# First FFN matmul of a dense top-2 MoE block: weights loaded one chunk at a time, and the two token halves of a chunk interleaved

## The chip, the cores and the metric

One Trainium2 chip, 8 cores. Each core runs the same program on its own batch element (x has the shape 8 x 2048 x 1024); the cores share nothing but read the same weights. The metric is the device time of the slowest core, in microseconds (us). TensorE is PE in the rows, VectorE DVE, ScalarE ACT, GpSimd POOL and SyncE SP.

## The reference

Each token is normalised, goes through an attention block whose softmax weights the token's own value (so it is a value projection and an output projection), and through a mixture of 8 experts with top-2 routing. Every expert is computed for every token; the routing weights pick two of them afterwards.

```python
def _L0_ffn_ref(hidden_states, router_w, w1, b1, w2, b2):
    router_logits = jnp.einsum('bth,eh->bte', x, router_w)
    topk_values, topk_indices = jax.lax.top_k(router_logits, TOP_K)
    topk_weights = jax.nn.softmax(topk_values.astype(jnp.float32), axis=-1).astype(x.dtype)
    h1 = jnp.einsum('bth,efh->btef', x, w1) + b1
    h1 = jax.nn.gelu(h1, approximate=False)
    expert_outputs = jnp.einsum('btef,ehf->bteh', h1, w2) + b2
    ...
xn = _layernorm(x, axis=-1)
x = x + _L0_attn_ref(xn, ...) + _L0_ffn_ref(xn, ...)
```

Per core: 2048 tokens, width 1024, 8 experts, inner width 4096.

## The kernel before

The program is written as five streams of instructions, one for each engine, with semaphores between them that the code sets by hand (class Plan, lines 26 to 65). The order on each engine is the order in which the code emits. All matmuls are bf16 into fp32 PSUM; the weights lie in memory as fp32 and are cast to bf16 by the DMAs that POOL issues.

**Stages.** emit_A (line 210) normalises 128 tokens, transposes them into xnF and computes the routing weights; it runs 16 times. emit_vproj (line 169) is the value projection, once for four tiles of tokens. The FFN goes over two halves of 1024 tokens, and in each half over the 8 experts e. For one half and one expert, emit_h1 (line 355) computes h1 in 16 groups g of two chunks f1c (32 chunks of 128 inner columns), and emit_w2 (line 386) then takes those chunks through w2 in two sweeps hh of 512 output columns each. In the first half, expert 0's 16 groups of h1 are mixed between the calls of emit_A for the tiles 8 to 15 (lines 475 to 479). emit_outproj (line 359) stands before w2 of expert 0 in each half. emit_final (line 447) adds x and the result and stores it; its loads and stores are issued by SP.

**One group of h1, emit_h1_group, line 316.** One DMA on POOL's queue (line 321) loads both chunks of the group: 128 partitions x 2 chunks x 1024 values, 512 KB as they arrive in bf16, into one of two slots of w1sl (slot g % 2, 2048 columns each). Before it, POOL waits until the last matmul that read this slot is done (line 319). Each chunk then has 16 matmuls (line 338): 8 slices fc of the width 1024, for each of two halves j of the 1024 tokens, 512 tokens each. The stationary operand is the 128x128 block fc of the chunk's weights, the moving one 512 tokens of xnF, and j names the PSUM bank of the chunk's pair of banks (SP[f1c % 2], P01 or P23). j is the outer loop and fc the inner one, so the 8 blocks are gone through once for j = 0 and once more for j = 1. Before the first matmul of a chunk, PE waits for the DMA (line 328), for ACT to have read the pair two chunks earlier (wait_pair, line 329), and where needed for the readers of vg (line 333). Behind the last matmul ACT takes Gelu over both banks into vg (line 350).

**One group of w2, line 389.** One 256 KB DMA (line 396) into one of four slots, then 2 chunks x 8 token tiles = 16 matmuls (line 419), each into one of the eight PSUM banks, with another stationary block for every matmul.

**emit_outproj** (line 369) has fc outer and j inner: the same stationary block of optF stands in two matmuls one after the other, which write the two banks of a pair.

POOL's queue holds, in this order, the w1 DMAs of an expert, the w2 DMAs of both sweeps, the w1 DMAs of the next expert, and so on; a DMA that waits holds up all behind it.

Of the kernel before, what the change touches and what calls it, by code (L numbers as in the profile page):

```python
# [17 lines left out]
NFC = 8  # L18
# [49 lines left out]
def build_nc(phases="ABC", dbg=False):  # L68
# [8 lines left out]
    d_w1 = nc.dram_tensor("w1r", [E, NF1C, 128, NFC, 128], F32, kind="ExternalInput").ap()  # L77
# [14 lines left out]
    w1sl = wvw[:, 0:4096]  # L92
# [15 lines left out]
    if dbg:  # L108
# [12 lines left out]

    p = Plan(nc)
    p.mksem("pe", "act", "dve", "dx0", "dx1", "dq0", "dq1", "dw1a", "dw1b",
            "dw2a", "dw2b", "dw2c", "dw2d", "dcst", "dwv", "dwo", "do0", "do1",
            "ddbg")
    DX = ("dx0", "dx1")
    DQ = ("dq0", "dq1")
    DW1 = ("dw1a", "dw1b")
    DW2 = ("dw2a", "dw2b", "dw2c", "dw2d")
    DO = ("do0", "do1")  # L130

# [10 lines left out]
    for fc in range(NFC):  # L142
        p.do("gpsimd", lambda g, fc=fc: g.dma_start(
            wo_sb[:, fc * 1024:(fc + 1) * 1024], d_wo[fc * 128:(fc + 1) * 128, :]),
            inc="dwo", inc_by=16)
# [12 lines left out]
    def wait_pair(pidx):  # L158
        if pair_last[pidx] is not None:
            sem, tok = pair_last[pidx]  # L160
            p.wait("tensor", sem, tok)

    def set_pair(pidx, sem, tok):
        pair_last[pidx] = (sem, tok)
# [136 lines left out]
            emit_vproj(tt // 4)  # L301


    nw1 = {0: 0, 1: 0}
    nw2 = {0: 0, 1: 0, 2: 0, 3: 0}
    tok_w1use = {}
    tok_w2use = {}
# [6 lines left out]
    tok_w2_reader = {}  # L314

    def emit_h1_group(half, e, g):
        sl = g % 2
        if tok_w1use.get(sl) is not None:
            p.wait("gpsimd", "pe", tok_w1use[sl])
        nw1[sl] += 1  # L320
        p.do("gpsimd", lambda gg, e=e, g=g, sl=sl: gg.dma_start(  # L321
            w1sl[:, sl * 2048:(sl + 1) * 2048].rearrange(
                "p (c m) -> p c m", c=2),
            d_w1[e, 2 * g:2 * g + 2].rearrange("c p f n -> p c (f n)")),
            inc=DW1[sl], inc_by=16)
        for f1c in (2 * g, 2 * g + 1):
            pair = SP[f1c % 2]
            p.wait("tensor", DW1[sl], 16 * nw1[sl])
            wait_pair(f1c % 2)
            if e == 0 and half == 0:  # L330
                p.wait("tensor", "dve", tok_xnFev[7])
            if tok_w2_reader.get(f1c) is not None:
                p.wait("tensor", "pe", tok_w2_reader[f1c])
            for j in range(2):
                for fc in range(NFC):
                    tok = p.do("tensor",
                               lambda t, fc=fc, f1c=f1c, j=j, sl=sl, half=half,
                               pair=pair: t.matmul(  # L338
                                   pair[:, j * 512:(j + 1) * 512],
                                   w1sl[:, sl * 2048 + (f1c % 2) * 1024 +  # L340
                                        fc * 128: sl * 2048 + (f1c % 2) * 1024 +
                                        fc * 128 + 128],
                                   xnF[:, fc * T + half * 1024 + j * 512:
                                       fc * T + half * 1024 + (j + 1) * 512],
                                   start=(fc == 0), stop=(fc == NFC - 1)),
                               inc=("pe" if (j == 1 and fc == NFC - 1) else None))
            tok_w1use[sl] = tok
            p.wait("scalar", "pe", tok)
            tok_gelu[(half, e, f1c)] = p.do(
                "scalar", lambda s, f1c=f1c, e=e, pair=pair: s.activation(  # L350
                    vg[:, f1c * 1024:(f1c + 1) * 1024], pair, AF.Gelu,
                    bias=b1c_sb[:, f1c * E + e: f1c * E + e + 1]), inc="act")
            set_pair(f1c % 2, "act", tok_gelu[(half, e, f1c)])

    def emit_h1(half, e):
        for g in range(NF1C // 2):
            emit_h1_group(half, e, g)
# [117 lines left out]
    for tt in range(8, NTT):  # L475
        if DO_C:
            emit_h1_group(0, 0, 2 * (tt - 8))
            emit_h1_group(0, 0, 2 * (tt - 8) + 1)
        emit_A(tt)
# [14 lines left out]
    if dbg:  # L494
# [6 lines left out]
        for dst, s_ in dumps:  # L501
            p.do("gpsimd", lambda g, dst=dst, s_=s_: g.dma_start(dst, s_),
                 inc="ddbg", inc_by=16)
# [75 lines left out]
```

How the kernel before makes its waits and increments, by code:

```python
    def wait(self, eng, name, val=None):  # L40
        v = self.cnt[name] if val is None else val
        if v <= 0 or self.waited[eng].get(name, -1) >= v:
            return
        self.waited[eng][name] = v
        s = self.sem[name]
        self.streams[eng].append(lambda En, s=s, v=v: En.wait_ge(s, v))
# [3 lines left out]
    def do(self, eng, fn, inc=None, inc_by=1):  # L50
        own = self.SELF_SEM.get(eng)
        if own is not None:
            self.wait(eng, own)
            if inc is None:
                inc, inc_by = own, 1
        if inc is None:
            self.streams[eng].append(fn)
            return None
        self.cnt[inc] += inc_by
        tok = self.cnt[inc]
        s = self.sem[inc]
        self.streams[eng].append(
            lambda En, fn=fn, s=s, n=inc_by: fn(En).then_inc(s, n)
        )
        return tok
```

## Time and profile before

| what | value |
|---|---|
| runs shown | 4741.36 and 4861.77 us, median 4801.57 us |
| the profiled execution | 4190.35 us, of which its span (first to last instruction of the slowest core, core 5) is 4188.8 us |
| spans of the 8 cores | 4149.0 to 4188.8 us |
| mean granted TensorE clock | 0.957 on core 5, 0.957 to 0.966 over the cores |
| PE busy | 3809.2 us, 91% of the span |
| POOL busy | 575.3 us, 14% |
| DMA | 307.02 MB moved, 73 GB/s on the mean |

The profile is of one execution, on the slowest of its cores. Matmuls are pipelined, and the end of each is modelled: one takes 379 ns in the records, but the next starts 216 ns after it. Idle time counts only where the engine with the work waits; for this kernel that is PE.

### The profile page before, as it was taken

What the parts mean: (1) busy time and instruction counts of PE and PEld (TensorE: products, weight loads), DVE (VectorE), ACT (ScalarE), POOL (GpSimd) and SP (SyncE); (2) the same over time, 40 slices, a digit from 0 to 9 for tenths busy, and PEclk for the clock granted to TensorE, in tenths of its full rate; (3) what the DMA queues carried; (4) which work ended last, traced back from release to release, by engine and by line L of the source; (5) the groups of instructions that cost most, each with busy time, mean ns of one, the idle gap of its engine ahead of it and who ended that gap; (6) DMA issues with size and microseconds to landing.
All of it is one profiled execution on the core that took longest, in us unless ns stands there. A gap on an engine that the chain in (4) does not pass through costs nothing.

```text
span 4188.8 us, 41300 instructions; the slowest of 8 cores (4149.0 to 4188.8 us)
## 1 busy us (share of the span) xinstructions
PE 3809.2 (91%) x17200; PEld 1692.3 (40%) x17200; DVE 372.6 (9%) x626; ACT 626.8 (15%) x610; POOL 575.3 (14%) x817
## 2 busy tenths in 40 slices
PE   3456799999999999999999999999999999999994
PEld 1222344444444444444444444444444444444442
DVE  3331100000001010000001000000000010100001
ACT  0122103021111202030201103020111202030200
POOL 1001010111111111111111011111111111111110
PEclk9677899999999999999999999999999999999986
DMA  4334254544454544544456354445454444454443
GB/s 75 53 54 73 29 78 66 73 74 73 74 78 71 76 70 76 78 71 71 76 73 138 62 75 75 69 73 74 74 77 72 77 69 76 72 81 67 75 67 99
DMA packets 251605, 307.02 MB, mean 73 GB/s; under 512 B 47591, under 2 KB 178663, under 8 KB 251424
## 3 DMA queue, kind: packets, MB, share of 16 engines
q0 software_dynamic: 244512, 279.21, 45.2%
q1 hardware_dynamic: 6912, 25.17, 1.8%
q8 instruction: 141, 2.31, 0.2%
q14 instruction: 40, 0.33, 0.0%
HBM read 574.89 MB, written 8.39 MB: 139 GB/s over the span
## 4 chain that ended last, share of the span: by engine, by line
PE 84%; DMA 6%; DVE 6%; issue 2%; ACT 1%; DVEq 0%; POOL 0%; SPq 0%; ACTq 0%; POOLq 0%
PE P L419 41%; PE P L338 39%; DMA wvw<-w1r 4%; DVE scr L433 3%; PE P L369 1%; PE P L188 1%; DMA wvw<-wvf 1%; PE P L247 1%; DMA x_rot<-x 1%; ACT vg L350 1%; DVE xnF L253 0%; DMA b1c_sb<-b1c 0%; DVE scr L239 0%; DVEq L46 0%; ACT L232 0%
## 5 line engine op out<-in xcount | busy, mean ns | idle before, releaser
L419 PE MATMUL P<-wvw,vg 128*128 128x512 bf16 x8192 | 1833.1, 385 | 65.0 <-DVE scr L433 49.2
L338 PE MATMUL P<-xnF,wvw 128*128 128x512 bf16 x8192 | 1787.6, 381 | 29.4 <-DMA wvw<-w1r 22.5
L419 PEld LDWEIGHTS P<-wvw,vg 128*128 128x128 bf16 x8192 | 806.7, 99 | 1088.8 <-issue 201.2
L338 PEld LDWEIGHTS P<-xnF,wvw 128*128 128x128 bf16 x8192 | 800.4, 98 | 1014.9 <-issue 66.4
L350 ACT ACTIVATE vg<-P,b1c_sb 128x1024 bf16<-128x1024 f32 x512 | 570.5, 1114 | 2876.1 <-PE P L338 2876.0
L396 POOL DMA_DIRECT2D wvw<-w2r x512 | 359.8, 705 | 1600.8 <-PE P L419 1535.0
L433 DVE SCALAR_TENSOR_TENSOR scr<-P,wmap_sb,scr 128x512 f32<-128x512 f32 x256 | 192.1, 750 | 3284.6 <-PE P L419 3260.5
L321 POOL DMA_DIRECT2D wvw<-w1r x256 | 180.0, 704 | 1664.1 <-PE P L338 1664.1
L188 PE MATMUL P<-xnF,wvw 128*128 128x512 bf16 x256 | 85.1, 501 | 40.6 <-DMA wvw<-wvf 40.6
L247 PE MATMUL P<-scr 128*128 128x128 f32 x128 | 30.0, 413 | 98.2 <-DVE scr L239 80.9
L188 PEld LDWEIGHTS P<-xnF,wvw 128*128 128x128 bf16 x256 | 29.4, 120 | 94.6 <-issue 83.0
L294 PE MATMUL P<-scr,wmap_sb 128*8 128x128 f32 x16 | 5.9, 372 | 66.6 <-DVE wmap_sb L290 66.6
L178 POOL DMA_DIRECT2D wvw<-wvf x32 | 28.2, 885 | 278.3 <-PE P L188 278.3
L247 PEld LDWEIGHTS P<-scr 128*128 128x128 f32 x128 | 24.1, 216 | 104.5 <-issue 104.5
L369 PE MATMUL P<-wo_sb,optF 128*128 128x512 bf16 x256 | 58.0, 380 | 1.0 <-ACT optF L197 1.0
L350 ACT ACT_TABLE_LOAD x9 | 11.5, 1283 | 207.1 <-PE P L338 207.1
L197 ACT ACTIVATE optF<-P,bvc_sb 128x512 bf16<-128x512 f32 x32 | 22.0, 687 | 114.6 <-PE P L188 114.6
L369 PEld LDWEIGHTS P<-wo_sb,optF 128*128 128x128 bf16 x256 | 23.8, 98 | 34.1 <-issue 7.4
L382 DVE COPY scr<-P 128x1024 f32<-128x1024 f32 x16 | 19.6, 1225 | 140.9 <-PE P L375 140.9
L239 DVE TENSOR_SCALAR scr<-x_rot,scr 128x1024 f32<-128x1024 f32 x16 | 13.0, 812 | 206.0 <-ACT scr L234 206.0
L262 PE MATMUL P<-rout_sb,xnF 128*128 128x8 bf16 x128 | 5.7, 168 | 25.4 <-DVE xnF L253 25.4
L294 PEld LDWEIGHTS P<-scr,wmap_sb 128*8 128x8 f32 x16 | 1.3, 83 | 67.5 <-issue 67.5
(40 smaller groups left out, 194.7 us busy)
## 6 DMA issues: line engine op xcount, KB each, us to landing
wvw<-w1r POOLq DMA_DIRECT2D x256, 512.0 KB, 5.2
wvw<-w2r POOLq DMA_DIRECT2D x512, 256.0 KB, 4.2
x_rot<-x SPq DMA_DIRECT2D x32, 512.0 KB, 4.3
wvw<-wvf POOLq DMA_DIRECT2D x32, 256.0 KB, 4.8
out<-x_rot SPq DMA_DIRECT2D x16, 512.0 KB, 3.6
wo_sb<-wo POOLq DMA_DIRECT2D x8, 256.0 KB, 11.0
b1c_sb<-b1c POOLq DMA_DIRECT2D x1, 128.0 KB, 12.8
scr<-iden POOLq DMA_DIRECT2D x1, 64.0 KB, 6.1
```

Of the source, the lines that this page charges most:

```text
L178: p.do("gpsimd", lambda g, vc=vc, sl=sl: g.dma_start(wvf_sl[:, sl * 1024:(sl + 1) * 1024].rearrange("p (c n) -> p c n", c=NFC), d_wvf[vc]. ...
L188: t.matmul(vps, wvf_sl[:, sl * 1024 + fc * 128: sl * 1024 + (fc + 1) * 128], xnF[:, fc * T + ts * 512: fc * T + (ts + 1) * 512], start=(fc ...
L197: s.activation(optF[:, vc * T + ts * 512: vc * T + (ts + 1) * 512], vps, AF.Identity, bias=bvc_sb[:, vc:vc + 1]), inc="act")
L247: tok = p.do("tensor", lambda t, fc=fc, xnt_t=xnt_t: t.transpose(P67[:, fc * 128:(fc + 1) * 128], xnt_t[:, fc * 128:(fc + 1) * 128], iden_ ...
L321: p.do("gpsimd", lambda gg, e=e, g=g, sl=sl: gg.dma_start(w1sl[:, sl * 2048:(sl + 1) * 2048].rearrange("p (c m) -> p c m", c=2), d_w1[e, 2 ...
L338: pair=pair: t.matmul(pair[:, j * 512:(j + 1) * 512], w1sl[:, sl * 2048 + (f1c % 2) * 1024 + fc * 128: sl * 2048 + (f1c % 2) * 1024 + fc * ...
L350: "scalar", lambda s, f1c=f1c, e=e, pair=pair: s.activation(vg[:, f1c * 1024:(f1c + 1) * 1024], pair, AF.Gelu, bias=b1c_sb[:, f1c * E + e: ...
L369: p.do("tensor", lambda t, fc=fc, tt=tt, j=j, pair=pair: t.matmul(pair[:, j * 512:(j + 1) * 512], optF[:, fc * T + tt * 128: fc * T + (tt ...
L382: v.tensor_copy(mixed[:, tl * 1024:(tl + 1) * 1024], pair), inc="dve")
L396: p.do("gpsimd", lambda gg, e=e, g=g, hh=hh, sl=sl: gg.dma_start(w2sl[:, sl * 1024:(sl + 1) * 1024].rearrange("p (c n) -> p c n", c=2), d_ ...
L419: t.matmul(W2B[tl], vg[:, f1c * 1024 + tl * 128: f1c * 1024 + (tl + 1) * 128], w2sl[:, sl * 1024 + (f1c % 2) * 512: sl * 1024 + (f1c % 2) ...
L433: v.scalar_tensor_tensor(mixed[:, tl * 1024 + hh * 512: tl * 1024 + hh * 512 + 512], W2B[tl], wmap_sb[:, tt * E + e: tt * E + e + 1], mixe ...
```

## The change

The change does three things, all in emit_h1_group.

- The DMA of a group is cut into two, one for each chunk, 256 KB each, and w1sl into four slots of 1024 columns (slot f1c % 4) with a semaphore each (dw1a to dw1d). The bytes in SBUF are as before. Each DMA waits for the last reader of its own slot, four chunks earlier; both DMAs of a group are issued ahead of the group's matmuls in the code.
- PE waits for each chunk's own DMA.
- The loops over fc and j change places: fc is outer, j inner, so that one stationary block stands in two matmuls one after the other.

```diff
+    DW1 = ("dw1a", "dw1b", "dw1c", "dw1d")
     def emit_h1_group(half, e, g):
-        sl = g % 2
-        if tok_w1use.get(sl) is not None:
-            p.wait("gpsimd", "pe", tok_w1use[sl])
-        nw1[sl] += 1
-        p.do("gpsimd", lambda gg, e=e, g=g, sl=sl: gg.dma_start(
-            w1sl[:, sl * 2048:(sl + 1) * 2048].rearrange(
-                "p (c m) -> p c m", c=2),
-            d_w1[e, 2 * g:2 * g + 2].rearrange("c p f n -> p c (f n)")),
-            inc=DW1[sl], inc_by=16)
         for f1c in (2 * g, 2 * g + 1):
+            sl = f1c % 4
+            if tok_w1use.get(sl) is not None:
+                p.wait("gpsimd", "pe", tok_w1use[sl])
+            nw1[sl] += 1
+            p.do("gpsimd", lambda gg, e=e, f1c=f1c, sl=sl: gg.dma_start(
+                w1sl[:, sl * 1024:(sl + 1) * 1024],
+                d_w1[e, f1c].rearrange("p f n -> p (f n)")),
+                inc=DW1[sl], inc_by=16)
+        for f1c in (2 * g, 2 * g + 1):
+            sl = f1c % 4
             pair = SP[f1c % 2]
             p.wait("tensor", DW1[sl], 16 * nw1[sl])
...
-            for j in range(2):
-                for fc in range(NFC):
+            for fc in range(NFC):
+                for j in range(2):
                     tok = p.do("tensor",
...
-                                   w1sl[:, sl * 2048 + (f1c % 2) * 1024 +
-                                        fc * 128: sl * 2048 + (f1c % 2) * 1024 +
-                                        fc * 128 + 128],
+                                   w1sl[:, sl * 1024 + fc * 128:
+                                        sl * 1024 + fc * 128 + 128],
```

On PE this is the beginning of h1 of expert 1 in the first half, right behind the w2 sweeps of expert 0. dw1a to dw1d are the semaphores of the w1 DMAs, dve those of the last sweep's sums, act the Gelus, pe the readers of vg. Before:

```order
L338 MATMUL P<-xnF,wvw 128x512 [waits dw1a,dve]
L338 MATMUL P<-xnF,wvw 128x512 x15
L338 MATMUL P<-xnF,wvw 128x512 [waits dve,pe]
L338 MATMUL P<-xnF,wvw 128x512 x15
L338 MATMUL P<-xnF,wvw 128x512 [waits dw1b,act]
L338 MATMUL P<-xnF,wvw 128x512 x15
L338 MATMUL P<-xnF,wvw 128x512 [waits act,pe]
L338 MATMUL P<-xnF,wvw 128x512 x15
```

The same place in the changed kernel, where the matmul's line is 339:

```order
L339 MATMUL P<-xnF,wvw 128x512 [waits dw1a,dve]
L339 MATMUL P<-xnF,wvw 128x512 x15
L339 MATMUL P<-xnF,wvw 128x512 [waits dw1b,dve,pe]
L339 MATMUL P<-xnF,wvw 128x512 x15
L339 MATMUL P<-xnF,wvw 128x512 [waits dw1c,act]
L339 MATMUL P<-xnF,wvw 128x512 x15
L339 MATMUL P<-xnF,wvw 128x512 [waits dw1d,act,pe]
L339 MATMUL P<-xnF,wvw 128x512 x15
```

Every chunk of 16 matmuls, and not every second, now waits for a DMA; the number of matmuls and their shapes stay.

On POOL this is the end of a w2 sweep pair, the w1 DMAs of the next expert, and the beginning of its w2. Before:

```order
L396 DMA wvw<-w2r 128x2x512
L396 DMA wvw<-w2r 128x2x512 [waits pe] x28
L321 DMA wvw<-w1r 128x2x1024 x2
L321 DMA wvw<-w1r 128x2x1024 [waits pe] x14
L396 DMA wvw<-w2r 128x2x512 x4
L396 DMA wvw<-w2r 128x2x512 [waits pe] x28
```

And in the changed kernel, where the DMA's line is 322:

```order
L396 DMA wvw<-w2r 128x2x512
L396 DMA wvw<-w2r 128x2x512 [waits pe] x28
L322 DMA wvw<-w1r 128x1024 x4
L322 DMA wvw<-w1r 128x1024 [waits pe] x28
L396 DMA wvw<-w2r 128x2x512 x4
L396 DMA wvw<-w2r 128x2x512 [waits pe] x28
```

The 16 w1 DMAs of an expert become 32 of half the size; 4 in place of 2 are issued without a wait, and they hold the same four chunks. What stands before and behind them keeps its place.

## Rows read from the trace of the kernel before

**Rows 1.** The page: span, and busy time (share, count) of each engine.

```profile
span 4188.8 us, 41300 instructions; the slowest of 8 cores (4149.0 to 4188.8 us)
PE 3809.2 (91%) x17200; PEld 1692.3 (40%) x17200; DVE 372.6 (9%) x626; ACT 626.8 (15%) x610; POOL 575.3 (14%) x817
```

**Rows 2.** The page: groups; count | busy us, mean ns | idle before, releaser.

```profile
L419 PE MATMUL P<-wvw,vg 128*128 128x512 bf16 x8192 | 1833.1, 385 | 65.0 <-DVE scr L433 49.2
L338 PE MATMUL P<-xnF,wvw 128*128 128x512 bf16 x8192 | 1787.6, 381 | 29.4 <-DMA wvw<-w1r 22.5
...
L338 PEld LDWEIGHTS P<-xnF,wvw 128*128 128x128 bf16 x8192 | 800.4, 98 | 1014.9 <-issue 66.4
...
L321 POOL DMA_DIRECT2D wvw<-w1r x256 | 180.0, 704 | 1664.1 <-PE P L338 1664.1
...
L369 PE MATMUL P<-wo_sb,optF 128*128 128x512 bf16 x256 | 58.0, 380 | 1.0 <-ACT optF L197 1.0
...
L369 PEld LDWEIGHTS P<-wo_sb,optF 128*128 128x128 bf16 x256 | 23.8, 98 | 34.1 <-issue 7.4
```

**Rows 3.** The waits of core 5: who <- for whom: us, times, longest.

```profile
PE P L419 <- DVE scr L433: 49.2, 95, 1.1
...
PE P L338 <- DMA wvw<-w1r: 22.5, 26, 2.6
```

**Rows 4.** The waits of core 1, whose span is 4149.0 us.

```profile
PE P L338 <- DMA wvw<-w1r: 9.4, 13, 1.7
```

**Rows 5.** Timeline, 632 to 662 us: h1 of expert 1; idle before in brackets.

```profile
632.01 13.97 PE L338 MATMUL P<-xnF,wvw 128*128 128x512 bf16 x64 [0.77 <-DVE scr L433]
...
639.63 0.70 POOL L321 DMA_DIRECT2D wvw<-w1r  x1 [19.53 <-PE P L338]
...
646.28 14.09 PE L338 MATMUL P<-xnF,wvw 128*128 128x512 bf16 x64 [0.30 <-DMA wvw<-w1r]
646.53 0.71 POOL L321 DMA_DIRECT2D wvw<-w1r  x1 [6.20 <-PE P L338]
```

**Rows 6.** Timeline, 478 to 500 us: PE in emit_outproj.

```profile
479.87 3.61 PE L369 MATMUL P<-wo_sb,optF 128*128 128x512 bf16 x16 [0.98 <-ACT optF L197]
```

**Rows 7.** The w1 DMAs by their line: who waited, and issue to landing.

```profile
L321 POOL DMA_DIRECT2D wvw<-w1r x256: 696/707/737, 188.4 to 3987.5; - x128
...
  PE P L338: 22.5, 26
...
DMA to landing us min/median/max: 5.0/5.2/9.3
```

**Rows 8.** The w2 DMAs the same way; nothing stands under "who waited".

```profile
L396 POOL DMA_DIRECT2D wvw<-w2r x512: 696/707/745, 472.0 to 4119.1; - x171
...
who waited for it (us, times):
busy tenths in 40 slices 0000010101010010101010010101010010101010
DMA to landing us min/median/max: 3.9/4.2/8.9
```

**Rows 9.** Timeline, 2228 to 2345 us: h1 at the start of the second half.

```profile
2280.75 0.70 POOL L321 DMA_DIRECT2D wvw<-w1r  x1 [8.23 <-PE P L338]
...
2287.65 0.71 POOL L321 DMA_DIRECT2D wvw<-w1r  x1 [6.21 <-PE P L338]
2289.65 0.61 PEld L338 LDWEIGHTS P<-xnF,wvw 128*128 128x128 bf16 x4 [3.04 <-issue]
2289.68 15.66 PE L338 MATMUL P<-xnF,wvw 128*128 128x512 bf16 x64 [2.57 <-DMA wvw<-w1r]
```

**Rows 10.** Windows of core 5, PE alone: busy (count), granted clock, DMA share, GB/s.

```profile
868.00:954.00 86.00, 86.00 (x400) 1.00 0.47 74
4075.00:4130.00 55.00, 55.00 (x212) 0.81 0.40 57
2281.00:2289.00 8.00, 6.10 (x29) 1.00 0.82 192
2290.00:2293.00 3.00, 3.00 (x9) 0.52 0.89 160
```

**Rows 11.** The chain that ended last, in order of time: start, us, what.

```profile
3773.16 53.48 PE P L419 x247
...
4068.64 65.46 PE P L419 x244
```

More of the change, by code:

```diff
@@ L123, in build_nc @@
     p.mksem("pe", "act", "dve", "dx0", "dx1", "dq0", "dq1", "dw1a", "dw1b",
-            "dw2a", "dw2b", "dw2c", "dw2d", "dcst", "dwv", "dwo", "do0", "do1",
-            "ddbg")
+            "dw2a", "dw2b", "dw2c", "dw2d", "dw1c", "dw1d", "dcst", "dwv",
+            "dwo", "do0", "do1", "ddbg")
     DX = ("dx0", "dx1")
     DQ = ("dq0", "dq1")
-    DW1 = ("dw1a", "dw1b")
+    DW1 = ("dw1a", "dw1b", "dw1c", "dw1d")
     DW2 = ("dw2a", "dw2b", "dw2c", "dw2d")
@@ L301, in emit_A @@
             emit_vproj(tt // 4)
-    nw1 = {0: 0, 1: 0}
+    nw1 = {0: 0, 1: 0, 2: 0, 3: 0}
     nw2 = {0: 0, 1: 0, 2: 0, 3: 0}
```

## The prediction

> **What bounds the kernel now.** I read the engines' busy times first. PE is busy for 3809.2 of 4188.8 us, and no other engine reaches 16% [rows 1]. The groups then say which matmuls these are: the two FFN lines, 8192 matmuls each, hold 1833.1 and 1787.6 us [rows 2]. The change touches line 338 alone, so the question is how much slack its 1787.6 us and the idle time before it hold.
>
> A busy PE need not be at its best pace, so next comes the timeline. Where h1 runs without a stop, 64 matmuls take 13.97 us [rows 5]; the last record is some 0.38 us long [rows 2], so one starts (13.97 - 0.38) / 63 = 215.7 ns after the other. At the granted clock of 1.00, which is the level of 2.4 GHz [rows 10], 512 columns need 512 / 2.4 = 213.3 ns. The stream is within 1.2% of one column each cycle. 8192 x 215.7 ns = 1767 us, so the 1787.6 us hold about 21 us that are not pace (drains in front of waits and matmuls at the lower clock), and idle time adds 29.4 us, of which 22.5 us stand against the w1 DMA, in 26 waits [rows 2, 3]. Were all of it to go, that is 50 us or 1.2%; this is the ceiling.
>
> **The 26 waits.** A w1 DMA is issued when the slot's second chunk is done, and it is needed one group later. Two rows show it: issue at 639.63, matmuls that need it at 646.28, after 0.30 us of idle time [rows 5]. The lead is 32 x 0.2157 = 6.9 us less the tail of the last matmul. The DMA lands after 5.2 us on the median and 9.3 at worst [rows 7], so most groups are not late, and the late ones are late by little. The worst stand at the start of the second half, where SP's loads and stores of emit_final share the DMA engines: issue at 2280.75, need met at 2289.68 after 2.57 us [rows 9], at a DMA share of 0.82 against 0.47 in a quiet stretch [rows 10].
>
> **Part 1, the split DMA and four slots.** A chunk's DMA is now issued when the chunk four before it is done, and three chunks lie between: the lead is 48 x 0.2157 = 10.4 us in place of 6.9. What does a 256 KB DMA take on this queue? The w2 line answers: 512 of them with four slots, one in every 16 matmuls, landing after 4.2 us on the median and 8.9 at worst, and PE waited for none [rows 8]. That is just the scheme that w1 gets, at the same cadence of 16 x 0.2157 = 3.45 us. So I let the 26 waits go. Each had idle time, and also a pipe that ran empty: the last record before it ends 379 - 216 = 163 ns past the time at which the next would have started. So the price is 22.5 + 26 x 0.163 = 26.7 us. The longest wait, with PE idle for 2.57 us, is followed by matmuls at the lower level of 1.2 GHz (clock 0.52 over 2290 to 2293; 64 matmuls take 15.66 in place of 13.97 us) [rows 9, 10], which adds 1.7 us. I leave about 3 us standing at the start of the second half, where DMA shares of 0.82 to 0.89 say that the engines are nearly full. Gain: about 25 us. Bounds: nothing, if all waits come back, and 28 us.
>
> What is late next behind these waits? ACT's Gelu and the last sweep's sums on DVE; neither gets nearer, since each chunk still has its 16 matmuls.
>
> The Trainium skill speaks against splitting: "DMA: Bandwidth & Descriptors", section "Rules for kernel authors", wants one large transfer, because each carries a fixed cost of about 2 us. The rows agree that halving does not halve the time (5.2 to 4.2 us) [rows 7, 8]; by that rule as by the rows the fixed part lies beside matmuls, and the sum stays.
>
> **Part 2, twice the issues.** 256 more issues on POOL at 704 ns are 180 us of POOL [rows 2], which is busy for 575.3 of 4188.8 us [rows 1]; an issue every 3.45 us leaves it 2.7 us of rest. Behind a waiting w1 DMA stand the w2 DMAs of the same expert; the last w1 DMA waits for chunk 27 as before, so they start no later than by one issue. Cost on the path: nothing; were the cover gone, 180 us.
>
> **Part 3, one more DMA wait for each second chunk on PE.** It is met long before, as that for ACT is, and such waits cost nothing visible: 400 matmuls of 25 chunks fill 86.00 of 86.00 us [rows 10], 215 ns each.
>
> **Part 4, fc outside, j inside.** The order shows as many matmuls as before. Does each keep its weight load? The output projection is written in the new order already and has 256 loads for 256 matmuls [rows 2]. A load takes 98 ns beside a matmul of 216 ns and lies under it; 16 matmuls in the new order take 3.61 us, (3.61 - 0.38) / 15 = 215 ns each [rows 6], and line 419 changes bank and block with each matmul at (53.48 - 0.38) / 246 = 215.9 ns [rows 11]. So neither alternating banks nor a block that stands twice moves the pace: 0 us. Bounds: 8192 x (215.7 - 213.3) = 20 us less, if the pace fell to the column count; and 401 us more, as in the first rival.
>
> **Sum.** 4190.35 - 25 = 4165 us against the profiled execution, 0.6% less. Core 1 had only 9.4 us of these waits [rows 4], so the slower cores gain more than the faster ones; core 5 stays near the top.
>
> The runs shown have a median of 4801.57 us, 611 us above that execution, and no row shows where they spend it. One row suggests it: in the last 130 us the granted clock is 0.81 [rows 10], and there 244 matmuls take 65.46 us, 268 ns each against 216 [rows 11], that is 1.24 times as long. The excess of 551 and 671 us would be about 2300 to 2800 us of work at that pace (551 / 0.24 and 671 / 0.24): an estimate. At that pace 32 matmuls are 8.6 us, and a DMA of 5 to 7 us is not late; what the waits cost there is nearly nil. If the first 1300 to 1800 us run at full clock, the change takes out the waits of that part alone, some 9 us, and 1 or 2 us later. So I forecast 4801.57 - 11 = 4790 us.
>
> **Rivals.**
>
> *Weight loads come out from under the matmuls (slower).* Place: the second matmul of each pair, whose load finds the same block. Price: 4096 x 98 ns = 401 us, 5190 us. It decides from 2% on, 96 us, which is 12 ns for each matmul of the line. Against it stand the 16 matmuls of 3.61 us [rows 6]. The Trainium skill's "TensorE: Matmul & The Clock Gate", section "The mechanism" of its part 3, lets a load overlap only where the row groups differ; by that it would be exposed in both kernels. The trace disagrees: 98 + 216 ns would be a pace of 314. Chance 0.02.
>
> *The two small DMAs are served one after the other (slower).* Then a pair takes 2 x 4.2 = 8.4 us against 6.9 us of matmuls, 1.5 us late for each of 256 groups, 384 us: 5170 us. It decides once a chunk's DMA takes over 3.8 us of the queue for itself. Against it: w2's DMAs have the same size and cadence, and no wait [rows 8]. Chance 0.02.
>
> *The clock steps down at another time.* The step to 0.81 stood near the end of the profiled execution and would stand halfway in the runs shown. If it comes 400 us of work earlier or later, that is 96 us, and the change needs no part in it: the two runs shown differ by 120 us. Later: 4690 us or less, down to 4165 if it hardly comes; chance 0.14. Earlier: 4890 us and up to 4165 + 0.24 x 3809 = 5080; chance 0.08. The Trainium skill's "TensorE: Matmul & The Clock Gate", section "Seeing it yourself", has a peak-current limit that takes the clock to 13/16 soon after a third core of a die does dense work; by it nearly the whole run would be at 0.81, the 5080 us. The trace disagrees: clock 1.00 at 868 us with eight cores at work [rows 10].
>
> *Fewer weight loads by reuse (faster).* Were the second load of each pair gone, 4096 loads would be gone that nobody waits for: 0 us, within the forecast.
>
> **How the numbers follow.** Forecast, within 2%: 0.74, with a range of its own from 4700 to 4875. Faster by over 2%: 0.14, all of it the clock, since 50 us is the ceiling of the change itself. Slower by over 2%: 0.08 + 0.02 + 0.02 = 0.12. 2% is about what a measurement of this kernel can tell from no change; its two runs lie 2.5% apart. For 8 in 10 the range runs from 4540, half of the clock's better side, to 4890.
>
> **What would show it.** Right: PE's waits for w1 fall from 26 to 5 or fewer and below 3 us; 8192 loads remain on the h1 line and 64 matmuls still take 13.97 us; 512 w1 DMAs land after about 4.2 us; POOL's busy time rises to some 755 us; the span falls by 20 to 28 us. Wrong: a pace of h1 away from 215.7 ns at clock 1.00, DMA waits of PE at every group, or fewer loads with a shorter time.

## The result, and the profile after

The changed kernel takes 0.9932 of the time before, with a 95% interval of 0.9919 to 0.9945: faster by 0.7%, which lies within the 2% that the prediction allows its forecast. The medians are 4156.43 us (11 runs, 4150.78 to 4759.68) and 4466.99 us (10 runs, 4179.22 to 4888.12). These medians are not the comparison: in some executions of either kernel the cores of a die are granted 0.81 of TensorE's clock (the lower grant) for part of the time, and the ratio is over the executions in which that did not happen, 4150.78 to 4157.18 us against 4179.22 to 4192.62.

First the page of the changed kernel, from the profiled execution of 4150.11 us (slowest core: 7): the span, the busy times and the groups that answer to [rows 1] and [rows 2].

```profile
span 4148.6 us, 42034 instructions; the slowest of 8 cores (4134.1 to 4148.6 us)
...
PE 3790.2 (91%) x17200; PEld 1690.6 (41%) x17200; DVE 372.5 (9%) x626; ACT 626.8 (15%) x610; POOL 667.0 (16%) x1073
...
L419 PE MATMUL P<-wvw,vg 128*128 128x512 bf16 x8192 | 1818.2, 383 | 65.6 <-DVE scr L433 49.9
L339 PE MATMUL P<-xnF,wvw 128*128 128x512 bf16 x8192 | 1782.2, 381 | 6.6 <-DVE scr L433 6.6
...
L339 PEld LDWEIGHTS P<-xnF,wvw 128*128 128x128 bf16 x8192 | 802.5, 98 | 984.2 <-issue 28.3
...
L396 POOL DMA_DIRECT2D wvw<-w2r x512 | 360.1, 706 | 1586.0 <-PE P L419 1513.6
L322 POOL DMA_DIRECT2D wvw<-w1r x512 | 271.3, 533 | 1546.1 <-PE P L339 1546.1
```

The h1 line kept its 8192 matmuls and its 8192 weight loads. What went is the idle time before it: 29.4 us in [rows 2], now 6.6 us, all of it the wait for the last sweep's sums, which was there before. The wait for w1 is no longer among the releasers. The DMAs' own rows say the same (they answer to [rows 7]):

```profile
L322 POOL DMA_DIRECT2D wvw<-w1r x512: 528/528/568, 187.5 to 3963.8; - x171
...
who waited for it (us, times):
busy tenths in 40 slices 0000001010000101010100001010000001010100
DMA to landing us min/median/max: 3.9/4.2/8.5
```

They are 512 now, land after 4.2 us on the median and 8.5 at worst, and nothing stands under "who waited". On the eight cores together one wait of 0.4 us is left, on core 6; before, each core had between 9.4 and 23.6 us.

The worst place before was the start of the second half [rows 9]. The timeline of PE in the changed kernel there, 2240 to 2320 us:

```profile
2239.64 80.67 PE L339 MATMUL P<-xnF,wvw 128*128 128x512 bf16 x373
```

One unbroken row: 372 steps in 80.67 - 0.38 us, 215.8 ns each. Before, the same stretch was six pieces with five waits between them, and one piece begun at the level of 1.2 GHz.

### The profiled spans fell by more than the ratio says

The slowest core's span fell by 40.2 us (4188.8 - 4148.6); the ratio says 0.68% of 4181, which is 28 us. Core 5, the slowest before, explains the difference. Its groups in the changed kernel:

```profile
L419 PE MATMUL P<-wvw,vg 128*128 128x512 bf16 x8192 | 1815.2, 383 | 66.4 <-DVE scr L433 50.7 <-ACT vg L350 13.7 <-DVE scr L382 2.0
L339 PE MATMUL P<-xnF,wvw 128*128 128x512 bf16 x8192 | 1781.8, 380 | 6.6 <-DVE scr L433 6.6
```

On this core the h1 line gave back 1787.6 - 1781.8 = 5.8 us of busy time and 29.4 - 6.6 = 22.8 us of idle time, 28.6 us together: this is the change. It is no peculiarity of core 5: busy and idle time of the h1 line together fall from 1817.0 to 1789.4 us on the mean of the eight cores, which is 27.6 us. Line 419, which the change doesn't touch, gave another 1833.1 - 1815.2 = 17.9 us. That is the granted clock: in the kernel before, core 5 ended at 0.80, as its window from 4029 to 4135 us shows (busy, matmuls, granted clock, DMA share, GB/s). Its last h1 matmuls are over by 4001 us, so none of the 28.6 us comes from there. In the changed kernel's profile no core is below 0.91 in any 40 us from 520 to 4080 us.

```profile
4029.00:4135.00 106.00, 103.42 (x388) 0.80 0.39 54
```

### The profile page after: what moved, and what is told of

Same layout as the page of the kernel before. It is cut to its first block, busy times and chain, and to the rows that moved or that the text cites. A ratio compares the mean times of both kernels' runs of the same rounds, so it can differ in the third digit from the quotient of the medians.

```text
span 4148.6 us, 42034 instructions; the slowest of 8 cores (4134.1 to 4148.6 us)
## 1 busy us (share of the span) xinstructions
PE 3790.2 (91%) x17200; PEld 1690.6 (41%) x17200; DVE 372.5 (9%) x626; ACT 626.8 (15%) x610; POOL 667.0 (16%) x1073
## 4 chain that ended last, share of the span: by engine, by line
PE 88%; DVE 6%; DMA 2%; issue 2%; ACT 1%; DVEq 0%; POOL 0%; SPq 0%; ACTq 0%; POOLq 0%
PE P L339 43%; PE P L419 42%; DVE scr L433 3%; DMA wvw<-wvf 1%; PE P L188 1%; PE P L369 1%; DMA x_rot<-x 1%; PE P L247 1%; ACT vg L350 1%; DVE xnF L253 0%; DMA b1c_sb<-b1c 0%; DVE scr L239 0%; DVEq L46 0%; ACT L232 0%; DVE x_rot L463 0%
## 5 line engine op out<-in xcount | busy, mean ns | idle before, releaser
L322 POOL DMA_DIRECT2D wvw<-w1r x512 | 271.3, 533 | 1546.1 <-PE P L339 1546.1
L188 PE MATMUL P<-xnF,wvw 128*128 128x512 bf16 x256 | 88.5, 517 | 41.3 <-DMA wvw<-wvf 41.2
L247 PEld LDWEIGHTS P<-scr 128*128 128x128 f32 x128 | 22.5, 204 | 103.7 <-issue 103.7
```

The costliest lines, as they stand in the source:

```text
L188: t.matmul(vps, wvf_sl[:, sl * 1024 + fc * 128: sl * 1024 + (fc + 1) * 128], xnF[:, fc * T + ts * 512: fc * T + (ts + 1) * 512], start=(fc ...
L247: tok = p.do("tensor", lambda t, fc=fc, xnt_t=xnt_t: t.transpose(P67[:, fc * 128:(fc + 1) * 128], xnt_t[:, fc * 128:(fc + 1) * 128], iden_ ...
L322: p.do("gpsimd", lambda gg, e=e, f1c=f1c, sl=sl: gg.dma_start(w1sl[:, sl * 1024:(sl + 1) * 1024], d_w1[e, f1c].rearrange("p f n -> p (f n)")),
```

## The experiments

Each time is a ratio to the kernel before, run on the same chip beside it.

**The split without the changed loops.** j is outside again; the DMAs, slots and waits are the changed kernel's.

```diff
-            for fc in range(NFC):
-                for j in range(2):
+            for j in range(2):
+                for fc in range(NFC):
```

> Split DMA and four slots, with the old loop order (j outside, fc inside). If the gain is the w1 DMAs' lead (my theory): 0.993 of before, waits of PE for w1 at most 2 on core 0 to 7 and under 1 us, pace of h1 215.8 ns. If the gain comes from the same block standing in two matmuls (rival): 1.000 of before.

This run gave no ratio (its profiled execution took 4152.57 us), so the same kernel was run once more.

> The split alone (old loop order) once more with more rounds, for its ratio. If the split is the whole gain: 0.993 of before, as the changed kernel. If the loops' order has a part: nearer to 0.996.

Measured in the second: 0.9942, interval 0.9924 to 0.996, which holds the changed kernel's 0.9932; in both profiles no core has a wait for w1. The ratio alone does not separate 0.993 from 0.996. The first profile says more: busy and idle time of the h1 line together are 1790.0 us on the mean of the eight cores, where the changed kernel has 1789.4 and the kernel before 1817.0.

**The changed loops without the split.** The reverse: the kernel before with fc outside and j inside.

```diff
-            for j in range(2):
-                for fc in range(NFC):
+            for fc in range(NFC):
+                for j in range(2):
```

> Only the loops change places; one 512 KB DMA for two chunks and two slots as before. My theory: 1.000 of before within 0.002, some 13 to 28 waits for w1 and 9 to 24 us of them on a core as in the rows of before, pace 215.8 ns with 8192 loads. Rival: 0.993, and a pace below 215.8 ns.

Here, too, the first run gave no ratio, and the kernel was run once more.

> The changed loop order alone once more with more rounds. If the order is worth nothing: 1.000 of before within 0.002. If it has a part in the gain: 0.997 or less.

Measured: 1.0001, interval 0.9991 to 1.0012. The group of the h1 line in its second profile (core 3, span 4175.7 us):

```profile
L338 PE MATMUL P<-xnF,wvw 128*128 128x512 bf16 x8192 | 1785.8, 380 | 24.8 <-DMA wvw<-w1r 16.6
```

The waits for w1 are back, 16.6 us on this core and 10.0 to 17.0 us over the eight. The order of the loops is worth nothing, to within 0.1%, as its part of the sum said. In this one profile the h1 line takes 1810.6 us on the mean of the cores, 6.4 less than in the profile before, but the ratio over the timed executions shows no gain. With the split alone at the changed kernel's level, the 0.7% is the split.

**The smaller DMA, with the old lead for the first chunk.** Both DMAs of a group are held until the whole group two before it is done. The second chunk, which is needed 16 matmuls later, keeps its 10.4 us.

```diff
-            if tok_w1use.get(sl) is not None:
-                p.wait("gpsimd", "pe", tok_w1use[sl])
+            if tok_w1use.get(sl | 1) is not None:
+                p.wait("gpsimd", "pe", tok_w1use[sl | 1])
```

> The changed kernel, but both DMAs of a group are issued only when the whole group two before it is done, as the one DMA was; so the first chunk keeps the old lead of 6.9 us and the second has 10.4 us. If the lead is what counts (as the prediction put it): most of the 26 waits come back, over 12 us of them, 0.996 to 1.000 of before. If the smaller DMA with a semaphore of its own is enough (rival: 256 KB land after 4.2 us and not 5.2): under 6 us of waits, 0.993 to 0.995.

Measured: 0.995, interval 0.9932 to 0.9967. Its waits on the slowest core (7), us, times, longest, and where on the timeline they stand:

```profile
PE P L339 <- DMA wvw<-w1r: 4.3, 3, 1.9
```

```profile
2257.57 34.79 PE L339 MATMUL P<-xnF,wvw 128*128 128x512 bf16 x160 [1.74 <-DMA wvw<-w1r]
2293.03 7.07 PE L339 MATMUL P<-xnF,wvw 128*128 128x512 bf16 x32 [0.68 <-DMA wvw<-w1r]
2301.98 18.29 PE L339 MATMUL P<-xnF,wvw 128*128 128x512 bf16 x84 [1.88 <-DMA wvw<-w1r]
```

The rival is right: 0.2 to 4.3 us of waits over the cores, not over 12. With the old lead a 256 KB DMA lands after 4.8 us on the median, in time for a need 6.9 us on. It is late at the start of the second half, beside SP's loads and stores, and hardly elsewhere: of the 23 waits on the eight cores 20 stand there, and the other three, on cores 2 and 4, are 0.2 to 0.3 us long.

**The longer lead without the smaller DMA.** The kernel before with a third slot.

```diff
-    w1sl = wvw[:, 0:4096]
-    wo_sb = A("wo_sb", [128, NFC * 1024], BF16).ap()
+    w1sl = wvw[:, 0:6144]
+    wo_sb = A("wo_sb", [128, 6 * 1024], BF16).ap()
...
-        sl = g % 2
+        sl = n_group[0] % 3
+        n_group[0] += 1
```

> The kernel before with one slot more: 512 KB DMAs as before, three slots, so a lead of 32 matmuls more (13.8 us in place of 6.9). The third slot's room is taken from the output projection's weights: its last two of eight blocks are not loaded and the first two used in their place. If a longer lead alone suffices: no waits for w1 but at the start of the second half, 0.993 to 0.994 of before. If the size of the DMA is what matters (rival): waits stay near 26, 0.998 or more.

Measured: 0.994, interval 0.9919 to 0.9962. Its w1 DMAs on core 7:

```profile
L323 POOL DMA_DIRECT2D wvw<-w1r x256: 696/707/735, 188.1 to 3962.1; - x128
...
  PE P L340: 0.4, 1
...
DMA to landing us min/median/max: 5.0/6.1/14.0
```

One wait of 0.4 us; 1.5 us is the most on any core. Against the expectation none of them stands at the start of the second half: all lie before 350 us, where h1 is mixed with emit_A. The DMAs land later than before on this core (6.1 us on the median for the 5.2 of [rows 7], 14.0 at worst for 9.3); why is not shown, and it does no harm with 13.8 us to go. The ratio rests on few executions, but the h1 line itself agrees. Its busy and idle time together, in the profiled executions, on the mean of the eight cores:

| kernel | h1 line, us | waits for w1 on a core, us |
|---|---|---|
| before | 1817.0 | 9.4 to 23.6 |
| changed loops alone | 1810.6 | 10.0 to 17.0 |
| smaller DMA, old lead for the first chunk | 1792.4 | 0.2 to 4.3 |
| longer lead, 512 KB DMA | 1790.7 | 0 to 1.5 |
| split alone | 1790.0 | 0 |
| changed kernel | 1789.4 | 0 to 0.4 |

So either half of the change nearly does it alone, and the two do not add up.

**Twice as many DMAs again.** Each chunk's DMA cut in two, 128 KB each.

```diff
-            p.do("gpsimd", ...
-                w1sl[:, sl * 1024:(sl + 1) * 1024],
+            for q in range(2):
+                p.do("gpsimd", ...
+                    w1sl[:, sl * 1024 + q * 512:sl * 1024 + (q + 1) * 512],
```

> The changed kernel with each chunk's DMA cut in two once more, 128 KB each and 1024 of them in place of 512, same slots and waits. If issues and a DMA's fixed part lie beside the matmuls (my theory): 0.993 of before, no waits for w1, POOL busy some 270 us more. If more and smaller DMAs are what costs (rival): waits for w1 come back, over 0.996.

Measured: 0.9932, interval 0.9907 to 0.9956, and no wait for w1 on any core. Its DMAs on core 5:

```profile
L323 POOL DMA_DIRECT2D wvw<-w1r x1024: 528/536/605, 183.8 to 3956.1; - x171
...
DMA to landing us min/median/max: 2.7/3.4/7.1
```

POOL spends 542.0 us on them in place of 271.3, and the time is the changed kernel's. In this kernel more and smaller DMAs cost nothing that ends up on PE's path.

This kernel's profile caught one die at the lower grant for nearly the whole execution. Spans and mean granted clocks of the cores, then the window from 868 to 954 us of core 3 and of core 5, each counted from the core's own first instruction (busy, matmuls, granted clock, DMA share, GB/s):

```profile
core 2: 4867.9 us, clock 0.806
core 3: 4860.3 us, clock 0.806
...
core 5: 4141.5 us, clock 0.963
...
die 0 (median of its cores): 4852.9 us, clock 0.806
die 1 (median of its cores): 4138.0 us, clock 0.964
```

```profile
868.00:954.00 86.00, 85.91 (x328) 0.81 0.45 64
```

```profile
868.00:954.00 86.00, 86.00 (x400) 1.00 0.54 77
```

One program, one execution, the same work on each core: die 1 is through after 4138 us, die 0 after 4853, 715 us more. The upper of the two runs that stood beside the kernel before, 4861.77 us, is at this level; the other, 4741.36, lies below it.

**What the lower grant hangs on.** The tokens are multiplied by zero as they leave PSUM, so half of the matmuls (h1 and the value projection) stream zeros.

```diff
-        tok_xnFev[tt] = p.do("vector", lambda v, tt=tt: v.tensor_copy(
+        tok_xnFev[tt] = p.do("vector", lambda v, tt=tt: v.tensor_scalar_mul(
             xnF.rearrange("p (c t) -> p c t", c=NFC)[:, :, tt * 128:(tt + 1) * 128],
-            P67.rearrange("p (c t) -> p c t", c=NFC)), inc="dve")
+            P67.rearrange("p (c t) -> p c t", c=NFC), 0.0), inc="dve")
```

> The changed kernel with the normalised tokens multiplied by zero as they are copied out of PSUM, so that h1 and the value projection stream zeros; every instruction and DMA stays. This asks what the level of 0.81 of the granted clock hangs on, which set the level of the two runs shown. If on what the matmuls' data make the array do (one theory): 0.81 in no core, and 0.993 of before as the changed kernel. If on the stream of instructions alone (rival): 0.81 in some executions as before. The pace at 1.00 should stay 215.8 ns in both.

Measured: 0.9939, interval 0.9923 to 0.9955; one of its six executions had die 0 at 0.84 to 0.85 on the mean and took 4688 us. So zeros in h1 do not rule the lower grant out. Whether they make it rarer, six executions cannot tell, and w2's matmuls still streamed weights. The execution of 4688 us has no trace, so in which stage the grant fell isn't known. What sets it off stays open.

**The same remedy one stage earlier.** In the changed kernel the value projection still waits for its weights (17 waits, 41.2 us on core 7). Its two slots become four, in room that w2 doesn't use yet.

```diff
-    wvf_sl = wvw[:, 6144:8192]
+    wvf_sl = wvw[:, 4096:8192]
...
-            sl = vc % 2
+            sl = vc % 4
...
-                elif DO_B and sl >= 2:
-                    p.wait("gpsimd", "pe", tok_vpmm[(3, 7)])
+                elif DO_B:
+                    p.wait("gpsimd", "pe", tok_vpmm[(3, 4 + sl)])
```

> The changed kernel, with the same remedy one stage earlier: the value projection's weights, which have two slots and cost PE 41.2 us of idle time in 17 waits, get four slots (the w2 slots, which are free until then). If the lead is too short there too: these waits fall below 15 us, and the time to 0.984 to 0.989 of before. If the DMA engines are the limit there (rival; 256 KB in 1.7 us of matmuls): waits over 30 us, 0.992 to 0.994.

Measured: 0.9829, interval 0.9808 to 0.985, a little better than expected and better than both kernels. The waits fell, but on the slowest core not below the 15 us that were expected: 16.6 us there, 9.7 to 16.6 over the cores. The group of the value projection, in the changed kernel (core 7) and then here (core 1):

```profile
L188 PE MATMUL P<-xnF,wvw 128*128 128x512 bf16 x256 | 88.5, 517 | 41.3 <-DMA wvw<-wvf 41.2
```

```profile
L188 PE MATMUL P<-xnF,wvw 128*128 128x512 bf16 x256 | 71.2, 441 | 16.6 <-DMA wvw<-wvf 16.6
```

Idle time falls by 24.7 us and busy time by 17.3 us; on the mean of the eight cores it is 29.4 and 12.6, 42.0 us either way. The second is the clock: a matmul of the same shape is 441 ns long on the mean and not 517. The four passes were granted 0.74, 0.84, 0.76 and 0.72 in the changed kernel and 1.00, 0.83, 0.77 and 0.86 here. In the second and the third pass 8 matmuls still take 3.17 and 3.57 us behind pauses of 4.59 and 3.21 us; behind pauses of up to 1.03 us they take 1.89. Some of the waits remain, as a DMA must come every 1.7 us here and lands after 6.9 us.

## Why the prediction was right or wrong

**The mechanism and its size: right.** The waits for w1 went, and nothing else of the change moved the time by more than the runs can tell. The first sum, 22.5 + 26 x 0.163 + 1.7 = 28.4 us, is what came out: 28.6 us on core 5's h1 line, 27.6 us on the mean of the cores, and 28 us by the ratio. The 3 us that I held back for the start of the second half were not needed; no core kept more than 0.4 us. Against the profiled execution, 4165 us were forecast and 4150.11 measured; the 15 us between them are the 3 us held back and, for the rest, core 5's end at the lower grant, which cost line 419 17.9 us and which the sum counted as if it would come again. That this end did not come again is luck, and no part of the change.

**The cause: right, but I named one half of it.** I put it on the lead of 10.4 us in place of 6.9. The runs show that the smaller DMA with a semaphore of its own does nearly all of it with the old lead for the first chunk (24.6 of the 27.6 us on the h1 line), and that the lead does nearly all of it at the old size (26.3 of 27.6). Most waits were short, under 1 us for a DMA that was a little late, and either half covers that. Beside SP's traffic the smaller DMA alone still leaves waits and the longer lead alone leaves none, so there it is the lead. Size and semaphore were not tried apart.

**The loop order and the weight loads: right.** 8192 loads remain, the pace is 215.8 ns before and after, and the order alone is 1.0001. The rival of exposed loads (5190 us) is out, and so is that of two small DMAs served one after the other (5170 us): twice as many again cost nothing. That rival's threshold was mis-added: 96 us over 512 chunks is 0.19 us each, so it would have decided from 3.45 + 0.19 = 3.64 us on and not from 3.8.

**POOL's busy time: off in size.** I forecast 755 us from 704 ns for each issue; it is 667.0, because the new DMA takes 528 ns to issue. It lay beside the matmuls either way.

**The time: wrong, and the range with it.** The step that failed is the last of the sum, "So I forecast 4801.57 - 11 = 4790 us". I took the median of two runs for the kernel's level, and explained the 611 us above the profiled execution by a clock that steps down halfway. That the excess is the lower grant holds: an execution of the kernel before that took 4760.24 us had die 0 at 0.827 to 0.830 on the mean and die 1 at 0.962 to 0.964. But it is not the kernel's usual level: of the ten executions of the kernel before, five took 4179 to 4193 us, which is the level of the profiled one, and of the eleven of the changed kernel seven took 4151 to 4157 us. Nor does the clock only step down: the last section shows a core that falls to the lower grant and comes back. The gain of 11 us fell with the same step; where the lower grant did not come, the whole 28 us showed.

The "clock" rival had that case ("down to 4165 if it hardly comes"), with a chance of 0.14 and outside a range that began at 4540. Its other end, 5080 us, was too high: a die at the lower grant throughout took 715 us more, and not 0.24 x 3809 = 914. With two levels known, one from the profile and one from the runs, and nothing in the trace to choose between them, the range had to hold both, from about 4150 to 4890. That the ratio lies within 2%, as the likeliest case said, it owes to the ceiling of 50 us and not to the level of 4790. The estimate of where the step comes has a slip too: 4190 less 2300 to 2800 us leaves 1390 to 1890 us at full clock, and not 1300 to 1800, which changes the 11 us by less than 1.

Whether the change bears on how often the lower grant comes, these counts cannot tell.

## What to carry to other kernels

A load's lead is the work between the release of its slot and its use, and not the number of slots: compare it with the landing times of the trace, and look at the largest and at the stretches where another queue is busy, not at the median. If PE runs at the pace of its columns everywhere, all that an edit of its loads can give is its idle time, plus the part of a drain at each wait, plus the matmuls at the 1.2 GHz level behind a long one; add these three up first. When the profiled execution and the timed runs lie as far apart as here (4190.35 and 4801.57 us), forecast the ratio from the trace, and let the range for the time hold both levels.

## What the runs showed of the hardware

- The issue of a DMA on POOL took longer with more blocks in its pattern, and hardly longer with more bytes. With one block for each partition it was 528 ns on the median for 256 KB (128 x 1024) and 536 for 128 KB (128 x 512); with two blocks 706 ns on the mean for 256 KB (128 x 2 x 512, w2 in the same kernel) and 704 for 512 KB (128 x 2 x 1024, w1 before); with eight blocks 873 on the median for 256 KB (128 x 8 x 128, the value projection). Twice the issues cost POOL 271.3 us where 180.0 stood before, so 1.5 times.
- The two dies of a chip were granted different clocks in one execution of one program: 0.81 on core 3 of die 0 and 1.00 on core 5 of die 1, 868 to 954 us into each core's span. At 0.81 there are 328 matmuls in the 86 us that hold 400 at 1.00.
- The lower grant also came back to the full one, and cores of one die had it at different points of the program. The first profile of the changed loops alone has these rows of the granted clock (tenths, in 40 slices of each core's own span), first core 0, then core 2 of the same die:

```profile
PEclk9667788888788899999999999999999999999997
PEclk9688999999999999999999999998888788888886
```

- PE waits less for DMAs where the clock is lower. In the same profile, from 3250 to 4200 us of each core's span, cores 2 and 3 were at 0.81 and had no wait for w1; cores 0, 1, 4 and 5 were at 0.99 and had 1.0 to 3.9 us in 2 to 7 waits.
